# GpSimd makes the high and low parts of the score maxima, first in its step, from two buffers of raw maxima

## The chip, the cores and the metric

One Trainium2 chip, one of its cores. The metric is the device time of one execution, in microseconds (us). Engines are named as in the profile: PE is TensorE, DVE is VectorE, ACT is ScalarE, POOL is GpSimd, SP is SyncE, which here only issues DMAs.

## The reference

A cross-attention block with an MLP, for 8 batches of 256 query rows and 256 context rows, width 512, 16 heads of 32, all in fp32:

```python
x = layer_norm(hidden_states, ln1_w, ln1_b)
q = x @ q_w + q_b                       # 16 heads of 32
k = encoder_hidden_states @ k_w + k_b
v = encoder_hidden_states @ v_w + v_b
attn = softmax(where(mask, q k^T * scale, min), axis=-1)
hidden = (attn v) @ cproj_w + cproj_b + residual
y = gelu(layer_norm(hidden, ln2_w, ln2_b) @ fc_w + fc_b)    # width 2048
return hidden + y @ proj_w + proj_b
```

## The kernel before

The kernel keeps fp32 precision by splitting each operand into a high and a low part and multiplying in three passes (high by high, high by low, low by high). It has two stages. The first does attention for all batches and takes about the first half of the span; the second does the MLP in four chunks of 512 rows and doesn't touch what is changed.

The attention stage is one software pipeline, written out by hand for each engine. A step (it, g) belongs to batch `it` and to group g of four heads, G = 4*it + g; there are 32 groups. Every engine runs the same list of steps in order, and they meet only by semaphores. Within a step the engines work on different groups:

- PE projects queries and keys of group G+3 (`project_qk`, lines 975 to 977), multiplies the scores of group G+2 with queries on the partitions (`scores`, L1009), turns the maxima of group G+1 (`transpose_max`, L1093), multiplies the scores of group G again with keys on the partitions and the row maxima subtracted (`transposed_scores`, L993), and multiplies probabilities by values for group G-1 (`values`, L1080 and L1082).
- DVE reduces the scores of group G+2 to negated row maxima, one reduction a head into `negm` (`maximum`, L731). After the fourth head it makes the high part in fp32r of those eight numbers a partition (a cast, L736) and the low part (a subtraction, L738), both into `m12`. `m_lo_done` tells PE.
- ACT takes the exponentials twice, once in fp32 into `p32` (L533) and once in fp16 into `p_hi` (L535), and copies the turned maxima to `mrow` (`maxima_out`, L574), which SP's queue then stores as three rows under the queries. `transposed_scores` of the next step waits for that DMA.
- POOL subtracts the two exponentials to `p_lo` (L462, four a step, which `values` of the next step waits for). ACT may be two of them ahead of POOL. At the end of the step with g = 1 POOL also adds the output bias to the two hidden tiles of the next batch (L470); between the second and the third `p_lo` come the attention output's division by the row sums (L455, g = 0) and the inverse standard deviation (L423, g = 2).

PE's order inside a step is what matters here. For g = 1, 2 and 3 `transpose_max` stands directly behind `project_qk` and the first pair of `transposed_scores`; for g = 0 it stands behind `values`, the context's transposes and the first scores. PE executes strictly in order, so whatever `transpose_max` waits for holds the rest of the step.

Of the kernel before, what the change touches and what calls it, by code (L numbers as in the profile page):

```python
# [29 lines left out]
fp32 = mybir.dt.float32  # L30
# [4 lines left out]
ALU = mybir.AluOpType  # L35
# [4 lines left out]
def xattn_kernel(nc, x, ctx_in, mask, ln1_w, ln1_b, q_w, q_b, k_w, k_b, v_w, v_b, c_w, c_b,  # L40
# [5 lines left out]
    P = 128  # L46
    KT = D // P
    TT = LQ // P
    KC = LK // P
    GH = P // HD  # L50
    NG = H // GH
# [16 lines left out]
    with ctx:  # L68

        def sb(name, shape, dt, offset):  # L70
            return nc.alloc_sbuf_tensor_at(name, shape, dt, offset=offset)
# [41 lines left out]
        vb_bc = sb("vb_bc", [P, D], fp32, A4 + 4 * KB)  # L113
        cb_bc = sb("cb_bc", [P, D], fp32, A4 + 6 * KB)
        A5 = A4 + 8 * KB
        negm = sb("negm", [P, TT, GH], fp32, A5)
        m12 = sb("m12", [P, TT, 3 * GH], fp32r, A5 + 32)
        rl = sb("rl", [P, TT, H], fp32, A5 + 160)
        mrow = sb("mrow", [3 * GH, LQ], fp32r, A5 + 288)
# [23 lines left out]
        psum = ctx.enter_context(nc.psum_tensor("psum", [P, 8, 512], fp32))  # L143
        ST, MX, PV, MS = 0, 2, 4, 6
# [21 lines left out]
        s = {n: ctx.enter_context(nc.semaphore(n)) for n in names}  # L166
# [6 lines left out]
        def wait(eng, sem, value):  # L173

            if not isinstance(value, int) or value > 0:
                eng.wait_ge(s[sem] if isinstance(sem, str) else sem, value)
# [4 lines left out]

        def group(G):
            return not isinstance(G, int) or 0 <= G < GROUPS

# [6 lines left out]
        def emptied(it, kind, n):  # L191

            if kind in ("qk", "m"):
                G = it * NG + n + (3 if kind == "qk" else 1)
                if not group(G):
                    return None
                return ("qk_lo_done", (G + 1) * 2) if kind == "qk" else ("mrow_ready", G + 1)
            b = it + {"v": 1, "att": -1, "c": -1 - n, "x": 2, "ctx": 1}[kind]
# [60 lines left out]

        def fills_upto(G, parity):  # L260

            if isinstance(G, int):
                return (G // 2 + 1) * FILLS if G >= 0 else 0
            return (G - parity) * (FILLS // 2) + FILLS
# [136 lines left out]
        @block.gpsimd  # L401
        def _(pool):
            def small(dst, src, sem):
                with nc.allow_non_contiguous_dma(reason="per-partition vectors, a few KB"):
                    pool.dma_start(dst, src).then_inc(s[sem], 16)

            def column(v):
                return v.rearrange("(k p) -> p k", p=P)

            def repeated(v):  # L410
                return v.rearrange("(o n) -> o n", o=1).to_broadcast([P, D])

            pool.memset(ident[:, :], 0.0).then_inc(s["ident_zero"], 1)
            pool.wait_ge(s["ident_zero"], 1)
            pool.affine_select(out=ident[:, :], in_=ident[:, :], compare_op=ALU.not_equal, fill=1.0,
                               base=0, pattern=[[-1, P]], channel_multiplier=1).then_inc(s["ident_ready"], 1)
            pool.memset(mhalf[:, :], -0.5).then_inc(s["pool_consts"], 1)
            pool.wait_ge(s["pool_consts"], 1)

            def inverse_std(b, n, var_sem, out_sem):  # L420

                wait(pool, var_sem, b + 1)
                pool.tensor_tensor(rstd[:, 0:n], vareps[:, 0:n], mhalf[:, 0:n], ALU.pow).then_inc(s[out_sem], 1)  # L423

            def constants():
                pool.memset(m12[:, :, :].bitcast(fp32), 0.0).then_inc(s["pool_consts"], 1)
                pool.memset(vparts[:, :, :, 0:1], 1.0).then_inc(s["pool_consts"], 1)
                pool.memset(maskrow[:, 0, :], 1.0).then_inc(s["pool_consts"], 1)
                pool.wait_ge(s["pool_consts"], 4)
                pool.memset(kst[3 * HD:3 * HD + 3, :, :].bitcast(fp32), 1.0).then_inc(s["pool_consts"], 1)  # L430
                pool.wait_ge(s["pool_consts"], 5)
                small(vb_bc[:, :], repeated(v_b), "small_loaded")
                small(cb_bc[:, :], repeated(c_b), "small_loaded")
                split_weight_lo(3)
                for dst, src in ((cols[:, LN2W:LN2W + KT], ln2_w), (cols[:, LN2B:LN2B + KT], ln2_b),
                                 (cols[:, FCB:FCB + FT], fc_b)):
                    small(dst, column(src), "mlp_columns_loaded")

            def split_weight_lo(n):

                pool.wait_ge(s["w_hi_act"], n - 1)
                pool.tensor_tensor(w_att[:, n, 1, :, :], w_att_raw[:, n, 1, :, :], w_att[:, n, 0, :, :].bitcast(fp32),
                                   ALU.subtract).then_inc(s["w_lo_pool"], 1)

            def step(it, g):
                G = it * NG + g
                for u in range(4):
                    if u == 2 and g == 2 and batch(it + 2):
                        inverse_std(it + 2, TT, "ln_var", "ln_rstd")
                    if u == 2 and g == 0 and batch(it - 1):  # L450
                        b = it - 1
                        wait(pool, "pv_taken", (b + 1) * 16)
                        for t in range(TT):
                            a = att[:, t, :].rearrange("p (h d) -> p h d", h=H)
                            pool.tensor_tensor(a, a, rl[:, t, :].rearrange("p (h o) -> p h o", o=1).to_broadcast([P, H, HD]),  # L455
                                               ALU.mult).then_inc(s["att_normed"], 1)
                    if group(G):

                        wait(pool, "p_hi_done", (G * 4) + (u + 1))
                        wait(pool, "pv_mm", (G - 1) * 2)  # L460
                        slot = (g % 2) * 4 + u
                        pool.tensor_tensor(p_lo[:, slot, :], p32[:, u % 2, :], p_hi[:, slot, :],  # L462
                                           ALU.subtract).then_inc(s["p_lo_done"], 1)
                if g == 1 and batch(it + 1):
                    b = it + 1
                    wait(pool, "x_normed", (b + 1) * 2)
                    wait(pool, "small_loaded", SMALL)
                    for t in range(TT):
                        h = hidden_tile(b * TT + t)
                        pool.tensor_tensor(h, h, cb_bc[:, :], ALU.add).then_inc(s["cb_added"], 1)  # L470

            def ln2(j):
                inverse_std(j, 1, "y_var", "y_rstd")

            def tail(it, g):
                if (it, g) == (B - 2, 3):
                    ln2(0)
                if it == B - 1 and g < 3:
                    ln2(g + 1)

            iterations(pool, step, weights=constants, tail=tail)

            def pb(j):
                wait(pool, "y_normed", j + 1)
                h = hidden_tile(j)
                pool.tensor_tensor(h, h, pb_bc[:, :], ALU.add).then_inc(s["pb_added"], 1)

            pool.wait_ge(s["pb_loaded"], 16)
            for t in range(CH):
                pb(t)  # L490

            def body(c, first):
                if has_next(c):
                    for t in range(CH):
                        ln2(c * CH + (CH + t))
                        pb(c * CH + (CH + t))

            chunks(pool, body)
# [194 lines left out]
        def _(dve):  # L693
# [28 lines left out]
            def maximum(it, g, heads):  # L722
                G = it * NG + g + 2
                if not group(G):
                    return
                if heads[0] == 0:
                    wait(dve, "m_lo_done", G)
                for h in heads:
                    n = G * 4 + h
                    wait(dve, "max_mm", n + 1)  # L730
                    dve.tensor_reduce(out=negm[:, :, h:h + 1], in_=psum[:, MX + h % 2, :].rearrange("p (t k) -> p t k", t=TT),  # L731
                                      axis=AX.X, op=ALU.max, negate=True).then_inc(s["max_taken"], 1)
                if heads[-1] == GH - 1:
                    wait(dve, "max_taken", (G + 1) * 4)
                    wait(dve, "m_tr", G)
                    dve.tensor_copy(m12[:, :, GH:2 * GH], negm[:, :, :]).then_inc(s["m_hi_done"], 1)  # L736
                    wait(dve, "m_hi_done", G + 1)
                    dve.tensor_tensor(m12[:, :, 2 * GH:3 * GH], negm[:, :, :], m12[:, :, GH:2 * GH].bitcast(fp32),  # L738
                                      ALU.subtract).then_inc(s["m_lo_done"], 1)

            def statistics(b, tiles, stats_sem, mv_sem, var_sem):
                n = len(tiles)
# [487 lines left out]
```

## Time and profile before

| | |
|---|---|
| median of 3 runs | 763.83 us (758.85 to 768.42) |
| profiled execution | 762.24 us, its span 760.4 us, mean granted clock 0.971 |
| PE busy | 700.5 us (92% of the span) |
| DVE busy | 464.7 us (61%) |
| ACT busy | 321.7 us (42%) |
| POOL busy | 251.7 us (33%) |
| attention stage | up to about 400 us, some 42.6 to 44.4 us a batch |

Busy time is summed over instructions. A row of the timeline gives the start, the length, and in brackets the engine's idle time just ahead of it with what ended that; an instruction that waited for something has no bracket if its engine was idle for less than 0.15 us.

### The profile page before, as it was taken

How to read it: one execution, taken by the hardware profiler on the slowest of the kernel's cores; microseconds unless marked ns; L12 is line 12 of the kernel's file. 1: busy time of each engine (PE TensorE's matmuls, PEld its weight loads, DVE VectorE, ACT ScalarE, POOL GpSimd, SP SyncE). 2: the span in 40 equal slices, each digit the busy share in tenths (PEclk: the TensorE clock that was granted, in tenths of full speed). 3: DMA queues.
4: the chain of work that ended last, by engine and by line, in shares of the span. 5: the costliest groups of instructions: out<-in, count | busy, mean ns of one | idle time of the engine just before them, and what ended most of it. 6: DMA issues, size and time to landing. Idle time of an engine off the chain costs nothing.

```text
span 760.4 us, 13145 instructions
## 1 busy us (share of the span) xinstructions
PE 700.5 (92%) x4544; PEld 607.7 (80%) x4544; DVE 464.7 (61%) x860; ACT 321.7 (42%) x581; POOL 251.7 (33%) x217
## 2 busy tenths in 40 slices
PE   2789989899999989899689999999999999999998
PEld 2678879798888979798567888888888888888886
DVE  5567978978888888978858675432225233251213
ACT  4337766767676676857652211112211121211110
POOL 3505556655646656656653111000000001000000
PEclk9888989999999999999889999999999999999999
DMA  9655654644555554444604400010001000010001
GB/s 249 209 168 142 169 163 127 174 114 149 147 167 140 154 157 123 112 129 141 181 1 149 142 1 1 1 55 1 1 0 56 0 0 0 0 55 1 1 0 57
DMA packets 51130, 69.16 MB, mean 91 GB/s; under 512 B 8328, under 2 KB 29192, under 8 KB 51088
## 3 DMA queue, kind: packets, MB, share of 16 engines
q1 hardware_dynamic: 50816, 68.07, 30.9%
q0 software_dynamic: 272, 0.54, 0.3%
q8 instruction: 25, 0.41, 0.2%
q14 instruction: 17, 0.14, 0.1%
HBM read 47.21 MB, written 20.99 MB: 90 GB/s over the span
## 4 chain that ended last, share of the span: by engine, by line
PE 71%; issue 9%; DVE 8%; POOL 6%; DMA 3%; ACT 2%; SPq 0%; DVEq 0%; ACTq 0%; POOLq 0%
PE psum L1172 8%; PE psum L1174 8%; PE psum L1173 8%; PE psum L1159 8%; PE psum L1158 8%; PE psum L1157 8%; PE psum L975 5%; PE psum L976 5%; PE psum L977 5%; POOL p_lo L462 5%; PE psum L1059 3%; PE psum L1009 2%; PE psum L993 2%; DVE negm L731 2%; DVE xn L833 1%
## 5 line engine op out<-in xcount | busy, mean ns | idle before, releaser
L462 POOL TENSOR_TENSOR p_lo<-p,p_hi 128x512 f16<-128x512 f32 x128 | 157.1, 1236 | 135.6 <-ACT p_hi L535 135.1
L662 ACT ACTIVATE h<-psum,cols 128x512 f32<-128x512 f32 x64 | 44.1, 690 | 290.1 <-PE psum L1159 290.0
L913 DVE CAST h_hi<-h 128x512 fp32r<-128x512 f32 x64 | 27.6, 431 | 207.4 <-ACT h L662 207.4
L533 ACT ACTIVATE p<-psum,maskbias 128x512 f32<-128x512 f32 x128 | 88.3, 690 | 44.8 <-PE psum L993 42.7
L1172 PE MATMUL psum<-w_mlp,h_hi 128*128 128x512 f32 x256 | 100.8, 394 | 0.9 <-DVE hidden L758 0.9
L1174 PE MATMUL psum<-w_mlp,h_lo 128*128 128x512 f32 x256 | 99.7, 390 | 0.0
L1173 PE MATMUL psum<-w_mlp,h_hi 128*128 128x512 f32 x256 | 99.7, 389 | 0.0
L1157 PE MATMUL psum<-y_hi,w_mlp 128*128 128x512 f32 x256 | 99.7, 389 | 0.0
L1159 PE MATMUL psum<-y_hi,w_mlp 128*128 128x512 f32 x256 | 99.6, 389 | 0.0
L1158 PE MATMUL psum<-y_lo,w_mlp 128*128 128x512 f32 x256 | 99.6, 389 | 0.0
L535 ACT ACTIVATE p_hi<-psum,maskbias 128x512 f16<-128x512 f32 x128 | 88.7, 693 | 0.0
L731 DVE TENSOR_REDUCE negm<-psum 128x2 f32<-128x512 f32 x128 | 81.5, 678 | 2.7 <-PE psum L1009 2.2
L423 POOL TENSOR_TENSOR rstd<-vareps,mhalf 128x1 f32<-128x1 f32 (+1 forms) x24 | 16.0, 669 | 179.1 <-DVE vareps L751 179.1
L1172 PEld LDWEIGHTS psum<-w_mlp,h_hi 128*128 128x128 f32 x256 | 48.1, 188 | 10.9 <-issue 1.3
L1174 PEld LDWEIGHTS psum<-w_mlp,h_lo 128*128 128x128 f32 x256 | 48.1, 188 | 10.1
L1158 PEld LDWEIGHTS psum<-y_lo,w_mlp 128*128 128x128 f32 x256 | 48.1, 188 | 10.0
L1159 PEld LDWEIGHTS psum<-y_hi,w_mlp 128*128 128x128 f32 x256 | 48.1, 188 | 10.0
L1157 PEld LDWEIGHTS psum<-y_hi,w_mlp 128*128 128x128 f32 x256 | 48.0, 188 | 10.0
L1173 PEld LDWEIGHTS psum<-w_mlp,h_hi 128*128 128x128 f32 x256 | 48.1, 188 | 9.6
L1009 PE MATMUL psum<-stacks 97*128 97x256 f32 x256 | 47.2, 307 | 8.4 <-DMA stacks<-qk_rows 6.1
L993 PE MATMUL psum<-stacks 99*128 99x256 f32 x256 | 44.4, 293 | 5.8 <-ACT p_hi L535 5.7
L1080 PE MATMUL psum<-vparts,p_hi 128*128 128x97 bf16 x512 | 45.1, 213 | 2.3 <-POOL p_lo L462 2.3
(104 smaller groups left out, 1511.3 us busy)
## 6 DMA issues: line engine op xcount, KB each, us to landing
qk_rows<-qk SPq DMA_DIRECT2D x32, 512.0 KB, 2.7
stacks<-qk_rows SPq DMA_DIRECT2D x64, 256.0 KB
stacks<-qk_rows SPq DMA_DIRECT2D x64, 128.0 KB
hidden<-in_x_dram SPq DMA_DIRECT2D x8, 512.0 KB, 4.4
ctx_sb<-in_ctx_dram SPq DMA_DIRECT2D x8, 512.0 KB, 5.1
w_mlp_raw<-in_L_xattn_fc_w_dram SPq DMA_DIRECT2D x16, 256.0 KB, 4.6
w_mlp_raw<-in_L_xattn_proj_w_dram SPq DMA_DIRECT2D x16, 256.0 KB, 6.3
out_dram<-hidden SPq DMA_DIRECT2D x16, 256.0 KB, 2.1
```

The source lines that it names most:

```text
L462: pool.tensor_tensor(p_lo[:, slot, :], p32[:, u % 2, :], p_hi[:, slot, :], ALU.subtract).then_inc(s["p_lo_done"], 1)
L533: act.activation(p32[:, u % 2, :], psum[:, ST + kc, :], ACT.Exp, bias=maskbias[:, kc:kc + 1], scale=SCALE32)
L535: act.activation(p_hi[:, (g % 2) * 4 + u, :], psum[:, ST + kc, :], ACT.Exp, bias=maskbias[:, kc:kc + 1], scale=SCALE32).then_inc(s["p_hi_d ...
L731: dve.tensor_reduce(out=negm[:, :, h:h + 1], in_=psum[:, MX + h % 2, :].rearrange("p (t k) -> p t k", t=TT), axis=AX.X, op=ALU.max, negate ...
L993: ins = nc.tensor.matmul(psum[:, ST + kc, hh * LQ:(hh + 1) * LQ], kst[0:SUBROWS, h, kc * P:(kc + 1) * P], qst[0:SUBROWS, h, :], start=True ...
L1009: ins = nc.tensor.matmul(psum[:, MX + hh % 2, t * LK:(t + 1) * LK], qst[0:MAXROWS, h, t * P:(t + 1) * P], kst[0:MAXROWS, h, :], start=True ...
L1157: nc.tensor.matmul(bank, w[:, 0, :], y_hi[:, k, :], start=(k == 0), stop=False)
L1158: nc.tensor.matmul(bank, w[:, 0, :], y_lo[:, k, :], start=False, stop=False)
L1159: ins = nc.tensor.matmul(bank, w[:, 1, :], y_hi[:, k, :], start=False, stop=(k == KT - 1))
L1172: nc.tensor.matmul(acc, h_hi[:, f % 2, cut], w_mlp[f][:, 2, :], start=(f == 0), stop=False)
L1173: nc.tensor.matmul(acc, h_hi[:, f % 2, cut], w_mlp[f][:, 3, :], start=False, stop=False)
L1174: nc.tensor.matmul(acc, h_lo[:, f % 2, cut], w_mlp[f][:, 2, :], start=False, stop=(f == FT - 1)).then_inc(s["proj_mm"], 1)
```

## The change

The two instructions that make the high and the low part go from the end of DVE's `maximum` to POOL, as the first thing of its step (`split_maxima`), so in the step after the one in which the maxima were taken. The high part is now an addition of `negm` to the first four columns of `m12`, which are zero since the start, instead of a cast. `negm` becomes two buffers, by the parity of the group, and DVE's wait before it overwrites one of them is for the group two back. PE's wait for `m_lo_done` is unchanged, and so is its place.

```diff
-        negm = sb("negm", [P, TT, GH], fp32, A5)
+        negm = [sb(f"negm{i}", [P, TT, GH], fp32, A5 + 128 * i) for i in range(2)]
...
+            def split_maxima(it, g):
+
+                G = it * NG + g + 1
+                if group(G):
+                    wait(pool, "max_taken", (G + 1) * 4)
+                    wait(pool, "m_tr", G)
+                    pool.tensor_tensor(m12[:, :, GH:2 * GH], negm[(g + 1) % 2][:, :, :], m12[:, :, 0:GH].bitcast(fp32),
+                                       ALU.add).then_inc(s["m_hi_done"], 1)
+                    wait(pool, "m_hi_done", G + 1)
+                    pool.tensor_tensor(m12[:, :, 2 * GH:3 * GH], negm[(g + 1) % 2][:, :, :], m12[:, :, GH:2 * GH].bitcast(fp32),
+                                       ALU.subtract).then_inc(s["m_lo_done"], 1)
+
             def step(it, g):
                 G = it * NG + g
+                split_maxima(it, g)
                 for u in range(4):
...
                 if heads[0] == 0:
-                    wait(dve, "m_lo_done", G)
+                    wait(dve, "m_lo_done", G - 1)
                 for h in heads:
                     n = G * 4 + h
                     wait(dve, "max_mm", n + 1)
-                    dve.tensor_reduce(out=negm[:, :, h:h + 1], in_=psum[:, MX + h % 2, :].rearrange("p (t k) -> p t k", t=TT),
+                    dve.tensor_reduce(out=negm[g % 2][:, :, h:h + 1], in_=psum[:, MX + h % 2, :].rearrange("p (t k) -> p t k", t=TT),
                                       axis=AX.X, op=ALU.max, negate=True).then_inc(s["max_taken"], 1)
-                if heads[-1] == GH - 1:
-                    wait(dve, "max_taken", (G + 1) * 4)
-                    wait(dve, "m_tr", G)
-                    dve.tensor_copy(m12[:, :, GH:2 * GH], negm[:, :, :]).then_inc(s["m_hi_done"], 1)
-                    wait(dve, "m_hi_done", G + 1)
-                    dve.tensor_tensor(m12[:, :, 2 * GH:3 * GH], negm[:, :, :], m12[:, :, GH:2 * GH].bitcast(fp32),
-                                      ALU.subtract).then_inc(s["m_lo_done"], 1)
```

## Rows read from the trace of the kernel before

**Rows 1.** Windows of one batch each: busy times of the engines, granted clock, DMA.

```profile
core 0: us, PE busy (x) PEld busy (x) DVE busy (x) ACT busy (x) POOL busy (x), PEclk, DMA share, GB/s
203.71:246.31 42.60, 39.64 (x370) 36.53 (x369) 37.35 (x71) 30.48 (x55) 25.59 (x22) 1.00 0.53 150
246.31:289.04 42.73, 39.78 (x370) 36.56 (x369) 37.47 (x71) 30.58 (x55) 25.58 (x22) 1.00 0.53 149
289.04:333.44 44.40, 41.40 (x370) 38.05 (x369) 37.53 (x71) 30.69 (x55) 25.62 (x22) 0.96 0.43 121
```

**Rows 2.** Waits of PE from 246 to 290 us: total us, times, longest.

```profile
PE psum L1093 <- DVE m L738: 1.7, 1, 1.7
PE psum L975 <- DVE cs L798: 0.8, 1, 0.8
PE psum L1009 <- DMA stacks<-qk_rows: 0.2, 1, 0.2
PE psum L1059 <- DVE hidden L758: 0.2, 1, 0.2
```

**Rows 3.** The tile of the parts: duration in ns, shortest, median and longest.

```profile
L736 DVE CAST m<-negm x32: 171/678/1071, 42.8 to 371.1; 128x8 fp32r<-128x8 f32 x32
L738 DVE TENSOR_TENSOR m<-negm,m x32: 166/1068/1126, 43.0 to 371.8; 128x8 fp32r<-128x8 f32 x32
```

**Rows 4.** Timeline of POOL in the batch from 246 us.

```profile
246.54 2.52 POOL L470 TENSOR_TENSOR hidden<-hidden,cb_bc 128x512 f32 x2
249.01 2.30 POOL L462 TENSOR_TENSOR p_lo<-p,p_hi 128x512 f16<-128x512 f32 x2
252.37 0.70 POOL L423 TENSOR_TENSOR rstd<-vareps,mhalf 128x2 f32<-128x2 f32 x1 [1.06 <-DVE vareps L751]
253.28 2.32 POOL L462 TENSOR_TENSOR p_lo<-p,p_hi 128x512 f16<-128x512 f32 x2 [0.20 <-ACT p_hi L535]
...
263.84 2.32 POOL L462 TENSOR_TENSOR p_lo<-p,p_hi 128x512 f16<-128x512 f32 x2 [3.60 <-ACT p_hi L535]
...
275.15 3.05 POOL L462 TENSOR_TENSOR p_lo<-p,p_hi 128x512 f16<-128x512 f32 x2
279.64 1.16 POOL L462 TENSOR_TENSOR p_lo<-p,p_hi 128x512 f16<-128x512 f32 x1 [1.44 <-ACT p_hi L535]
```

**Rows 5.** Timeline of DVE in the same batch.

```profile
252.12 0.17 DVE L751 TENSOR_SCALAR vareps<-mv 128x2 f32<-128x2 f32 x1
...
254.50 1.12 DVE L738 TENSOR_TENSOR m<-negm,m 128x8 fp32r<-128x8 f32 x1
...
269.69 0.69 DVE L798 TENSOR_TENSOR cs<-psum,cs 128x512 fp32r<-128x512 f32 x1 [0.78 <-ACT cs L542]
...
277.71 1.27 DVE L731 TENSOR_REDUCE negm<-psum 128x2 f32<-128x512 f32 x2
...
279.22 0.17 DVE L738 TENSOR_TENSOR m<-negm,m 128x8 fp32r<-128x8 f32 x1
```

**Rows 6.** Timeline of PE in the same batch: the turning of the maxima.

```profile
246.79 0.38 PE L1093 MATMUL psum<-ident,m 128*12 128x128 f32 x2
...
255.81 0.38 PE L1093 MATMUL psum<-ident,m 128*12 128x128 f32 x2
...
269.34 0.38 PE L1093 MATMUL psum<-ident,m 128*12 128x128 f32 x2
...
279.53 0.38 PE L1093 MATMUL psum<-ident,m 128*12 128x128 f32 x2 [1.69 <-DVE m L738]
```

**Rows 7.** Timeline of POOL elsewhere: instructions of other sizes.

```profile
11.36 0.75 POOL L405 DMA_DIRECT2D vb_bc<-in_L_xattn_v_b_dram  x1 [0.31 <-POOL stacks L430]
26.52 4.55 POOL L442 TENSOR_TENSOR w_att<-w_att_raw,w_att 128x2048 fp32r<-128x2048 f32 x1 [13.87 <-ACT w_att L515]
...
354.10 0.56 POOL L423 TENSOR_TENSOR rstd<-vareps,mhalf 128x1 f32<-128x1 f32 x1 [2.25 <-DVE vareps L751]
```

**Rows 8.** Waits of PE from 10 to 60 us.

```profile
PE psum L1009 <- DMA stacks<-qk_rows: 2.4, 1, 2.4
```

**Rows 9.** Windows: PE's busy time and granted clock behind that wait.

```profile
35.00:45.00 10.00, 9.11 (x50) 0.83 0.50 134
```

## The prediction

> **What bounds the kernel now.** I read the profile from the coarse to the fine. The table of busy times says PE, with 92% of the span. A window for each batch of the attention stage says the same there: 39.8 us of PE in a batch of 42.73 us, DVE 37.5, POOL 25.6 [rows 1]. So what PE doesn't wait for now can't be won. PE's waits in that batch add up to about 3 us, and only one of them, 1.7 us, has to do with the edited instructions [rows 2]. The two instructions look dear on DVE: the cast has a median of 0.68 us and the subtraction of 1.07 us, but their shortest are 0.17 each [rows 3]. The long ones end together with an instruction of POOL: the subtraction that starts at 254.50 ends at 255.62, when POOL's pair of low parts that started at 253.28 ends, at 255.60 [rows 4, 5]. They are stretched, not large. Some 0.68 + 1.07 - 2 x 0.17 = 1.4 us of DVE a step is such stretching, but DVE spends it at the end of a step in which nobody but PE's turning of the maxima waits for it.
>
> The third reading is a race: for each of the four steps of a batch, when PE gets to the turning of the maxima, when the last maximum is there, and when POOL comes free of the step before. I take the batch from 246.31 to 289.04; the two batches ahead of it show the same pattern to 0.1 us.
>
> **The change, part by part.**
>
> *DVE's two instructions leave.* In the steps with g = 2 and g = 3 DVE next works on what PE projects, and idles for it already, so nothing is won. In the step with g = 0 DVE would start about a microsecond earlier, but it waits again at 269.69 for ACT's context high part (0.78 us of idle) [rows 5], which follows PE; the lead is lost there, before the value split and the maxima that make PE's 1.7 us wait. I take nothing.
>
> *The price of the pair on POOL.* The trace has no small addition on POOL. From above: the power of two numbers a partition takes 0.70 us, of one 0.56 [rows 4, 7], and between an instruction of POOL and one that waits for it lie up to 0.31 us [rows 7]; with 0.25 between, that makes 1.65 us for the pair. From below: 2048 elements of subtraction take 4.55 us [rows 7], 512 of addition take 2.52/2 = 1.26 us [rows 4], so a line through them has a slope of 2.14 ns an element and begins at 0.16 us; two of 0.15 and 0.05 between make 0.35 us. Power is another operation and addition is the same one, so I take the value near the lower end: 0.20 + 0.15 + 0.20 = 0.55 us. PE starts 0.14 us after the low part is done (279.39 to 279.53) [rows 5, 6]. A gain from the pair itself is excluded: DVE's undisturbed pair takes 0.41 us, from 278.98 to 279.39 [rows 5], and starts without waiting for POOL.
>
> A rule of the Trainium skill speaks against this part of the change: "GPSIMD Engine Reference", section "Engine selection", gives elementwise work to VectorE, since GpSimd is about twice as slow with two inputs. Taken on DVE's undisturbed 0.17 us it would make the pair 2 x 0.34 + 0.15 = 0.83 us, an estimate by that page, and the sum below 19 x 0.28 = 5.3 us larger. It lies between my two ends, and the trace has no row that decides it.
>
> *The place: first in POOL's step, so behind everything of the step before.* Each step apart:
>
> - g = 2. POOL ends the step before with the two bias additions of the hidden tiles and comes free at 249.01; PE turned the maxima at 246.79 [rows 4, 6]. Now it can at 249.01 + 0.55 + 0.14 = 249.70, which is 2.91 us later. All seven batches that have these additions (g = 2 of batches 0 to 6) show it alike: 7 x 2.91 = 20.4 us.
> - g = 3. POOL comes free at 253.28 + 2.32 = 255.60; the turning goes from 255.81 to 255.60 + 0.69 = 256.29, 0.48 us [rows 4, 6]. POOL's third and fourth low parts follow PE's second pair of scores, so the distance stays even after the stall of g = 2. 7 x 0.48 = 3.4 us.
> - g = 0. POOL comes free at 263.84 + 2.32 = 266.16, PE turns at 269.34 [rows 4, 6]. Hidden, by 2.5 us.
> - g = 1. POOL is free at 275.15 + 3.05 = 278.20, ahead of the last maximum at 277.71 + 1.27 = 278.98 [rows 4, 5]. POOL starts 0.08 us after DVE's semaphore (252.29 to 252.37) [rows 4, 5], so PE turns at 278.98 + 0.08 + 0.55 + 0.14 = 279.75 instead of 279.53, 0.22 us. This race is open only from batch 2 on: 5 x 0.22 = 1.1 us.
>
> Sum of the stalls: 24.9 us. PE holds everything behind the turning: the values, the next scores, their maxima and the projections. ACT's copy of the turned maxima comes after the exponentials anyway, and SP's queue holds the fills of the stacks behind that copy's store, but both move by less than PE. Since PE stands still meanwhile, its waits for a fill and for DVE's hidden tile (0.2 and 0.2 us a batch [rows 2]) should vanish: 6 x 0.4 = 2.4 us back. POOL's queue has the low parts behind the new wait; at g = 1 they start at 279.64 after 1.44 us of idle [rows 4], and move by 0.1 us at most. The second buffer and DVE's earlier wait cost nothing: the old wait never showed as DVE's idle time. The tail, the last batch and the MLP chunks I take as unchanged.
>
> *The clock.* The last two batches shown differ by 44.40 - 42.73 = 1.67 us, at a clock of 0.96 against 1.00 and equal work [rows 1]: one fall to the lower level (1.2 of 2.4 GHz) costs 1.7 us. In the start of the kernel PE waited 2.4 us for a fill and the clock of the stretch behind it was 0.83 [rows 8, 9]. The 1.7 us wait at g = 1 was followed by a fall in the batch from 289 us and not in the two ahead of it. A stall of 2.9 us is longer than any of these, so I count a fall behind each: 7 x 1.7 = 11.9 us.
>
> A rule of the Trainium skill that speaks for the change: what DVE shows as 0.17 alone and 1.07 beside POOL, the page "Advanced Engine Details and Errata", "VectorE Performance Modes", puts to a port of DVE that is shared with POOL. The trace agrees. By that rule the release of DVE would be worth some 1.4 us in each of 32 steps if DVE bounded the stage; it doesn't, so it changes no term here.
>
> **The rivals.**
>
> *No fall of the clock.* The stalls come, but PE's clock stays. 762.24 + 24.9 - 2.4 = 784.7 us, and 781 with the shorter pair (19 turnings x 0.2 = 3.8 less). For it: two of the three batches shown took 1.7 us without a fall. Against it: the start of the kernel, and the length.
>
> *The pair is as slow as the power.* 1.1 us more at 19 turnings is 20.9 us, so 817.5 us. For it: the only small two-input instructions on POOL in the trace are 0.56 and 0.70 us. Against it: the line through the larger sizes.
>
> *PE's slack takes it.* If the fills, the accumulating products and the maxima are ahead of PE by more than the rows show, later steps run faster after a stall and half of it is lost: about 770 to 778 us. Against it: PE is 93% busy in the batch, and its other waits are 1.2 us.
>
> *The other side: DVE is the hidden bound.* The 1.7 us wait at g = 1 ends a chain through DVE (context low part, value split, maxima). If the microsecond released at the end of the step before got through that chain, PE would win up to 1.2 us in five batches, and the clock falls of two of them: 762 - 6 - 3.4 = some 753 us. It decides only where POOL is free before the last maximum, and that is so at g = 1 alone; at g = 2 POOL comes free 2.2 us after PE's turning whatever DVE does, so this needs the additions of the hidden tiles to be hidden too. Nothing in the rows says so. That the change fails to move the pair to POOL isn't possible; the additions with zero give the same numbers.
>
> **How the numbers follow.** Forecast, with the execution profiled: 762.24 + 24.9 - 2.4 + 11.9 = 796.6 us, say 796; it lies 1.6 us under the median of the runs shown, which is small beside the terms. Its own range is 788 to 806, for pairs of 0.35 to 0.9 us and five to eight falls; chance 0.50. No fall: 0.25. Slow pair: 0.11. Slack: 0.10. Faster: 0.04. The range from 778 to 816 leaves out the other side, the deeper half of the slack and the end of the slow pair. A change of less than 2% (under 779 and over 748 us) is about what a measurement of this kernel can't tell from none: chance 0.11. Slower by more: 0.86. Faster by more: 0.03.
>
> **What would show it.** In the profile after: 19 delayed turnings; a wait of PE's L1093 for POOL, some 2.9 us long in each of seven batches and about 0.5 in another step of each; batches of about 47 to 48 us; no wait at g = 0; POOL's new pair at 0.2 us each, directly behind L470 at g = 2; a clock under 0.97 in each batch; DVE's busy time in a batch about 5 us less, with no gain on PE. The prediction is wrong if POOL's small instructions cost 0.5 us or more, if the clock holds, or if PE catches up within the batch.

## The result

The changed kernel takes 794.0 us (median of 4 runs, 792.56 to 795.46); the kernel before takes 762.65 us (median of 4, the three above and one more). The ratio is 1.038, with a 95% interval from 1.034 to 1.043: slower by about 31 us. The forecast was 796 us. The profiled execution has a span of 790.8 us against 760.4.

In the page of the changed kernel, the table of busy times:

```profile
PE 708.5 (90%) x4544; PEld 613.0 (78%) x4544; DVE 434.1 (55%) x796; ACT 323.0 (41%) x581; POOL 271.3 (34%) x281
```

DVE has lost 64 instructions and 31 us of busy time, POOL has gained 64 and 20 us. PE runs the same 4544 products in 8 us more, and stands still for 22 us more. Those two numbers are the whole loss.

Windows of one batch each, to be laid beside [rows 1]:

```profile
216.45:263.28 46.83, 41.12 (x370) 37.57 (x369) 33.84 (x62) 30.63 (x55) 28.04 (x30) 0.96 0.48 136
263.28:311.88 48.60, 42.89 (x370) 39.37 (x369) 34.10 (x62) 30.75 (x55) 28.06 (x30) 0.93 0.46 131
311.88:358.55 46.67, 41.05 (x370) 37.64 (x369) 33.83 (x62) 30.69 (x55) 27.99 (x30) 0.96 0.40 115
```

A batch took 42.6 to 42.7 us where the clock held, and takes 46.7 to 48.6. The third field in front of the clock shows that DVE is 3.4 us less busy, and nobody is better off. PE's waits in the batch from 263.28 us, beside [rows 2]:

```profile
PE psum L1099 <- POOL m L454: 4.4, 2, 2.6
PE psum L981 <- DVE cs L804: 0.8, 1, 0.8
PE psum L1065 <- DVE hidden L764: 0.3, 1, 0.3
```

Line 1099 is the turning of the maxima. Its wait was for DVE, 1.7 us, once a batch; now it is for POOL, 4.4 us in two waits. The same batch in the timeline of POOL, beside [rows 4]:

```profile
263.50 2.49 POOL L483 TENSOR_TENSOR hidden<-hidden,cb_bc 128x512 f32 x2
265.95 0.21 POOL L451 TENSOR_TENSOR m<-negm,m 128x8 fp32r<-128x8 f32 x1
266.24 0.20 POOL L454 TENSOR_TENSOR m<-negm,m 128x8 fp32r<-128x8 f32 x1
266.40 2.27 POOL L475 TENSOR_TENSOR p_lo<-p,p_hi 128x512 f16<-128x512 f32 x2
...
300.19 0.20 POOL L451 TENSOR_TENSOR m<-negm,m 128x8 fp32r<-128x8 f32 x1 [0.85 <-DVE negm L744]
300.47 0.20 POOL L454 TENSOR_TENSOR m<-negm,m 128x8 fp32r<-128x8 f32 x1
```

and in the timeline of PE, beside [rows 6]:

```profile
266.50 0.38 PE L1099 MATMUL psum<-ident,m 128*12 128x128 f32 x2 [2.58 <-POOL m L454]
...
277.37 0.38 PE L1099 MATMUL psum<-ident,m 128*12 128x128 f32 x2
...
300.82 0.50 PE L1099 MATMUL psum<-ident,m 128*12 128x128 f32 x2 [1.86 <-POOL m L454]
```

DVE's last two maxima ahead of the first of these pairs are

```profile
260.36 1.29 DVE L744 TENSOR_REDUCE negm<-psum 128x2 f32<-128x512 f32 x2
```

At g = 2 the pair is ready to go when the last maximum is there, at 261.65 us, but POOL has low parts and then the bias additions of the hidden tiles ahead of it until 265.95. The pair itself takes 0.49 us. PE turns the maxima 0.06 us later, and had nothing to do for 2.58 us.

How late a turning is can be read against the start of PE's first scores of the same step, which doesn't depend on the pair. The windows above and those of [rows 1] begin at these scores, so at g = 2 the distance is 246.31 to 246.79 before and 263.28 to 266.50 now. From the timelines of PE at the steps with g = 2, 3 and 1, these distances were 0.48, 0.48 and 2.33 us, and are 3.22, 0.77 and 2.49. That is 2.74, 0.29 and 0.16 us more, at 7, 7 and 5 turnings: 19.2 + 2.0 + 0.8 = 22.0 us.

### The profile page after: what moved, and what is told of

It reads as the page before. It is cut to its first block, busy times and chain, and to the rows that moved or that the text cites. A ratio compares the mean times of both kernels' runs of the same rounds, so it can differ in the third digit from the quotient of the medians.

```text
span 790.8 us, 13144 instructions
## 1 busy us (share of the span) xinstructions
PE 708.5 (90%) x4544; PEld 613.0 (78%) x4544; DVE 434.1 (55%) x796; ACT 323.0 (41%) x581; POOL 271.3 (34%) x281
## 4 chain that ended last, share of the span: by engine, by line
PE 60%; issue 16%; POOL 9%; DVE 9%; ACT 3%; DMA 3%; SPq 0%; POOLq 0%; DVEq 0%; ACTq 0%
PE psum L1178 7%; PE psum L1180 7%; PE psum L1179 7%; PE psum L1163 7%; PE psum L1165 7%; PE psum L1164 7%; POOL p_lo L475 6%; PE psum L981 3%; PE psum L983 3%; PE psum L982 3%; POOL hidden L483 2%; DVE negm L744 2%; DVE vparts L851 2%; PE psum L1015 2%; DMA stacks<-qk_rows 1%
## 5 line engine op out<-in xcount | busy, mean ns | idle before, releaser
L1015 PE MATMUL psum<-stacks 97*128 97x256 f32 x256 | 50.1, 320 | 7.4 <-DMA stacks<-qk_rows 6.3
L778 DVE SCALAR_TENSOR_TENSOR qk<-psum,cols,qk 128x256 fp32r<-128x256 f32 x64 | 28.0, 478 | 52.4 <-ACT qk L579 52.3
L1086 PE MATMUL psum<-vparts,p_hi 128*128 128x97 bf16 x512 | 49.7, 222 | 2.2 <-POOL p_lo L475 2.2
```

The lines of the kernel that those rows point to most:

```text
L1015: ins = nc.tensor.matmul(psum[:, MX + hh % 2, t * LK:(t + 1) * LK], qst[0:MAXROWS, h, t * P:(t + 1) * P], kst[0:MAXROWS, h, :], start=True ...
L1086: nc.tensor.matmul(o, p_hi[:, slot, cut], vparts[:, kc, GH * gp + hh, :], start=(kc == 0), stop=False)
```

## The experiments

The time from the start of the kernel to batch 0 differs by up to 4.5 us between profiled executions whatever the kernel, and I haven't traced why. Where a microsecond matters I therefore compare the stretch between the same two events of the timeline: the start of the first scores with keys on the partitions in group 2, and the same in group 28. Before:

```profile
73.87:351.58 277.71, 258.00 (x2358) 0.98 0.50 144
```

The fields are the stretch, its length, PE's busy time and its granted clock. The changed kernel:

```profile
74.94:381.23 306.29, 267.63 (x2358) 0.94 0.46 131
```

28.6 of the 30.4 us by which the spans differ lie in this stretch, and PE is busy for 9.6 us more with the same 2358 products.

Two cautions hold for everything below. The kernel before was timed again beside each set of experiments, with medians of 766.51 (15 runs), 766.3 (29) and 767.15 us (16), some 4 us over the 762.65 us of the result; the changed kernel was timed only then. Each ratio is to the kernel before in the same set. And a trace is of one run, which can lie several us from the median of its kernel; where it does, I say so.

**The place: bias additions behind the pair.**

```diff
             def step(it, g):
                 G = it * NG + g
                 split_maxima(it, g)
+                if g == 2 and batch(it + 1):
+                    b = it + 1
+                    wait(pool, "x_normed", (b + 1) * 2)
+                    wait(pool, "small_loaded", SMALL)
+                    for t in range(TT):
+                        h = hidden_tile(b * TT + t)
+                        pool.tensor_tensor(h, h, cb_bc[:, :], ALU.add).then_inc(s["cb_added"], 1)
                 for u in range(4):
...
-                if g == 1 and batch(it + 1):
...
```

> The changed kernel with one thing moved: GpSimd's two bias additions of the hidden tiles stand behind the new pair (first thing of the step with g = 2) instead of ahead of it (last thing of the step with g = 1). Theory, the place: POOL comes free 2.5 us earlier, so the turning at g = 2 is late by 0.3 us instead of 2.7; 7 x 2.4 = 17 us of stall and some 10 us of clock falls go, and the time is 764 to 768 us, within 1% of the kernel before. Rival, the engine: small instructions on POOL, or POOL and DVE getting into each other's way, are the cost; then moving the additions gives back less than half, and the time stays over 780 us.

Measured 772.73 us, ratio 1.010 (1.006 to 1.013) to the kernel before. POOL's timeline and the stretch:

```profile
250.34 2.32 POOL L482 TENSOR_TENSOR p_lo<-p,p_hi 128x512 f16<-128x512 f32 x2 [3.19 <-ACT p_hi L548]
252.62 0.20 POOL L451 TENSOR_TENSOR m<-negm,m 128x8 fp32r<-128x8 f32 x1
252.90 0.20 POOL L454 TENSOR_TENSOR m<-negm,m 128x8 fp32r<-128x8 f32 x1
253.19 2.53 POOL L466 TENSOR_TENSOR hidden<-hidden,cb_bc 128x512 f32 x2
...
77.39:360.77 283.38, 260.94 (x2359) 0.97 0.51 142
```

The pair stands ahead of the additions, and the stretch is 283.4 us: 22.9 of the 28.6 us are gone. The same instructions run on the same engines, so the engine is not the cause; what POOL has to do first is. What is left is 5.7 us. The 0.3 us at g = 2 and g = 3, the 0.16 at g = 1 and one more fall of the clock would make 6.5; the difference isn't traced. The median is 5 us over the upper end of what I expected; the kernel before took 766.51 us beside it, where I had worked from 762.65, and that accounts for 4 of them.

**The buffer alone.**

```diff
-                    wait(dve, "m_lo_done", G)
+                    wait(dve, "m_lo_done", G - 1)
...
-                    dve.tensor_copy(m12[:, :, GH:2 * GH], negm[:, :, :]).then_inc(s["m_hi_done"], 1)
+                    dve.tensor_copy(m12[:, :, GH:2 * GH], negm[g % 2][:, :, :]).then_inc(s["m_hi_done"], 1)
```

The diff is against the kernel before; the maxima and the low part use the same buffer.

> The kernel before with the doubled buffer of the raw maxima and DVE's earlier wait, and the pair left on DVE. Theory: the second buffer frees nothing that anyone waits for, so the time is that of the kernel before within 0.3%. Rival: the old wait held the first maximum of each step; then this alone is faster by up to 32 x 0.1 = 3 us.

Measured 766.01 us, ratio 1.000 (0.996 to 1.003). By itself the second buffer brings nothing that can be told from the noise, and at most 2.8 us; it only makes room for the pair to be late. The stretch:

```profile
75.99:355.55 279.56, 258.78 (x2358) 0.98 0.51 143
```

That is 1.9 us more than in the trace of the kernel before, at the same time of the whole: differences of 2 us between two traces of this stretch mean nothing.

**The price of the pair: twice.**

```diff
                     wait(pool, "m_tr", G)
+                    pool.tensor_tensor(m_spare[:, :, 0:GH], negm[(g + 1) % 2][:, :, :], m12[:, :, 0:GH].bitcast(fp32),
+                                       ALU.add).then_inc(s["spare_hi"], 1)
+                    wait(pool, "spare_hi", G + 1)
+                    pool.tensor_tensor(m_spare[:, :, GH:2 * GH], negm[(g + 1) % 2][:, :, :], m_spare[:, :, 0:GH].bitcast(fp32),
+                                       ALU.subtract).then_inc(s["spare_lo"], 1)
+                    wait(pool, "spare_lo", G + 1)
```

> The changed kernel with the pair done twice on POOL, first into a spare tile and then as before, at the same place. Theory: POOL is what the turning waits for in 19 steps, so each is later by one more pair of 0.56 us (0.20 + 0.08 + 0.20 + 0.08), 10.6 us, and a few more falls of the clock of 1.7 us: 803 to 812 us. Rival, POOL isn't the last (PE waits for something else that ends with it): no change from 794.

Measured 812.71 us, ratio 1.062 (1.059 to 1.066). The stretch:

```profile
77.27:406.09 328.82, 280.57 (x2358) 0.89 0.43 122
```

PE's stall at g = 2 grows from 2.58 to 3.14 us, at g = 3 by 0.56 and at g = 1 by 0.55: each of the 19 turnings moves by exactly one pair, so all of them are bound by POOL. That is 10.6 us. The stretch is 22.5 us longer than the changed kernel's; the rest of that is the clock, now at 0.89, with PE busy for 12.9 us more. But this trace is of the slowest of the five runs, 5.1 us over the median. The medians lie 18.7 us apart, which leaves some 8 us for the clock; which of the two prices is the larger can't be told from this. The median is 0.7 us over the range that I expected.

**The clock by itself: PE is kept busy during the stall.**

```diff
                 if g == 2:
+                    if not isinstance(it, int) or 0 <= it < B - 1:
+                        wait(pe, "pv_taken", (it * NG + g - 2) * 4 + 2)
+                        for i in range(22):
+                            nc.tensor.matmul(psum[:, PV, GH * VW:GH * VW + 120], w_att[:, 2, 0, 0, 0:P],
+                                             w_att[:, 2, 0, 0, 0:120], start=True, stop=True)
                     transpose_max(it, g)
```

> The changed kernel with 22 matrix products of 120 columns, whose result nobody reads, ahead of the turning at g = 2 in batches 0 to 6, to keep PE busy in the 2.6 us in which it waits for POOL; they wait for nothing that is late. Theory, the clock: the stall itself stays, the falls that came with it in the trace of the changed kernel (a loss of some 10 us over the stage) go, so 784 to 788 us although PE does more. Rival, the clock cost nothing of its own (the falls would lie where PE has slack): 794, or more if the products last longer than the stall.

Measured 788.82 us, ratio 1.029 (1.024 to 1.034) against 1.038 (1.034 to 1.043) without the products. That is 0.8 us over the range that I expected and 5 us under the rival's; the two intervals just touch, so the trace has to decide. PE's timeline at one g = 2 and the stretch:

```profile
265.01 0.64 PE L999 MATMUL psum<-stacks 99*128 99x256 f32 x4
265.49 2.57 PE L1134 MATMUL psum<-w_att 128*128 128x120 f32 x22
268.25 0.39 PE L1099 MATMUL psum<-ident,m 128*12 128x128 f32 x2 [0.20 <-POOL m L454]
...
78.36:378.53 300.17, 278.81 (x2513) 0.97 0.48 133
```

PE executes 7 x 22 products more, starts each turning as late as the changed kernel does, and is 6.1 us faster over the stretch, with the clock at 0.97 instead of 0.94. The two are the same kernel but for the activity in the gap. The clock can be laid side by side: 10 us from the start of the first scores with keys on the partitions, in one step with g = 2, in the changed kernel, with the products, and with the pair done twice:

```profile
263.28:273.28 10.00, 7.42 (x61) 0.83 0.47 126
```

```profile
265.01:275.01 10.00, 9.80 (x96) 1.00 0.45 127
```

```profile
279.01:289.01 10.00, 6.86 (x52) 0.66 0.37 110
```

The granted clock is the same in all seven steps with g = 2 of each kernel: 0.83 with a gap of 2.58 us, 0.66 with one of 3.14 us, and 1.00 where the gap is filled. So the fall that comes with the stall has a price of its own, and where the stall was 0.56 us longer the loss of clock was double. The gain is somewhat under the 10 us that I expected: falls of the clock follow the 1.85 us waits at g = 1 in four of five batches here, and in two of five in the changed kernel.

**PE's order: the values fill the wait.**

```diff
                 if g == 2:
-                    transpose_max(it, g)
                     values(it, g)
+                    transpose_max(it, g)
...
                 if g == 3:
-                    transpose_max(it, g)
                     values(it, g)
+                    transpose_max(it, g)
```

> The changed kernel with PE's order alone altered: at g = 2 and g = 3 the values (some 1.2 us of PE) stand ahead of the turning of the maxima, where they fill the wait for POOL. Theory: the stall at g = 2 falls from 2.6 to about 1.4 us and the one at g = 3 goes, 7 x 1.5 = 10.5 us, and part of the clock falls with it: 776 to 784 us. Rival: the values or what follows the turning come late instead (the maxima's rows, the fills behind them), and the time stays within 3 us of 794.

Measured 772.67 us, ratio 1.010 (1.007 to 1.013), better than expected. The turning's row at g = 2 and the stretch:

```profile
255.12 0.38 PE L1099 MATMUL psum<-ident,m 128*12 128x128 f32 x2 [1.39 <-POOL m L454]
...
74.23:360.08 285.85, 254.65 (x2359) 0.99 0.49 139
```

The stall is 1.39 us, and the clock is at 0.99: in none of the seven steps with g = 2 did it fall. (The traced run is the fastest of the ten, 3.3 us under the median; its mean clock is 0.978, that of the others 0.969 to 0.978.) With POOL as late as in the changed kernel, 20.4 of the 28.6 us are gone: 7 x 1.19 = 8.3 us of stall at g = 2, 0.9 at g = 3 and 13.0 us of PE's busy time, less 1.9 us of longer waits for DVE's hidden tile. So the second condition of the loss is that nothing that PE could do stands in front of the turning.

**The tail.**

```diff
-            def tail(it, g):
-                if (it, g) == (B - 2, 3):
-                    ln2(0)
-                if it == B - 1 and g < 3:
-                    ln2(g + 1)
...
                 split_maxima(it, g)
+                if isinstance(it, int) and it == B - 1:
+                    ln2(g)
```

> The changed kernel with POOL's inverse standard deviations of the MLP's norm in the last batch put behind the new pair instead of ahead of it, because they wait for DVE and PE stood 4.2 us at the turning behind one of them. Theory from the step times: the last batch and what follows take only 0.8 us more in the changed kernel than before, so this stall lies where DVE is late anyway, and the time stays within 1.5 us of 794. Rival, the stall counts: 3 to 5 us less.

Measured 790.79 us, ratio 1.034 (1.028 to 1.040). In the changed kernel the longest single stall is in the last batch. PE's waits from 380 to 405 us:

```profile
PE psum L1099 <- POOL m L454: 6.0, 2, 4.2
```

POOL's inverse standard deviation for the MLP's norm is the last thing of a step there; it waits for DVE's statistics, and the pair is queued behind it. From the end of the stretch to the first product of the MLP's second matrix it is, in the changed kernel and in this one:

```profile
381.23:438.69 57.46, 44.42 (x333) 0.88 0.29 80
```

```profile
380.59:434.97 54.38, 43.36 (x333) 0.91 0.31 85
```

3.1 us less, where I had expected none and the rival 3 to 5. The intervals of the two ratios overlap, but three more traces have the inverse standard deviation ahead of the pair and PE's order as it was, those with the additions moved, the pair twice and the products in the gap; they took 58.4, 57.8 and 57.6 us for this piece. Against all four the gain is 3.1 to 4.0 us. The rival was right, and my argument that DVE is late there anyway was wrong. The kernel before and the one with the buffer alone took 56.7 and 54.7 us, so what the change costs in the tail is between 0.8 and 3.7 us, and no run here settles it closer.

**What the pair on DVE costs.** Two kernels made from the one before.

```diff
                 if g == 1:
+                    values(it, g)
                     transpose_max(it, g)
                     scores(it, g, (0, 1))
                     for j in range(2):
                         transposes(it, "att", j, it - 1, att, "att_normed", 2, "att_tr")
-                    values(it, g)
                     project_v(it, 0)
```

> The kernel before, with PE's values ahead of the turning of the maxima at g = 1, where PE waits 1.7 us for DVE's last maximum in five batches. Theory: the wait falls to some 0.4 us, 5 x 1.3 = 6.5 us, and the two clock falls behind it may go: 0.988 to 0.992 of the time before. Rival: PE's wait is only moved to the scores or to the transposes behind it, which wait for the same maxima: no change.

Measured 760.43 us, ratio 0.993 (0.991 to 0.996), a little less than expected. The turning waits no more. PE's waits over the stretch:

```profile
PE psum L975 <- DVE att_t L852: 6.1, 6, 1.1
PE psum L975 <- DVE cs L798: 4.0, 5, 0.8
PE psum L1080 <- POOL p_lo L462: 2.5, 5, 0.5
```

and the stretch:

```profile
77.82:352.64 274.82, 255.42 (x2358) 0.99 0.52 145
```

8.4 us of waiting for the maxima have become 6.1 for DVE's low part of the attention output and 2.5 for POOL. The wait was only moved, as the rival had it; of the 2.9 us that the stretch is shorter, 2.6 are PE's busy time, with a clock of 0.99 instead of 0.98.

```diff
-        negm = sb("negm", [P, TT, GH], fp32, A5)
-        m12 = sb("m12", [P, TT, 3 * GH], fp32r, A5 + 32)
+        m12 = [sb(f"m12_{i}", [P, TT, 3 * GH], fp32r, (A5 + 32, A5 + 544 + 3 * KB)[i]) for i in range(2)]
...
-                    dve.tensor_reduce(out=negm[:, :, h:h + 1], in_=psum[:, MX + h % 2, :].rearrange("p (t k) -> p t k", t=TT),
+                    dve.tensor_reduce(out=m12[g % 2][:, :, GH + h:GH + h + 1], in_=psum[:, MX + h % 2, :].rearrange("p (t k) -> p t k", t=TT),
                                       axis=AX.X, op=ALU.max, negate=True).then_inc(s["max_taken"], 1)
-                if heads[-1] == GH - 1:
...
-                wait(pe, "m_lo_done", G + 1)
+                wait(pe, "max_taken", (G + 1) * 4)
```

> The kernel before with no pair on any engine: DVE's maxima are written rounded straight into the high columns of a doubled tile, and the low part is left at zero (the softmax is the same whatever is subtracted). It shows what taking the pair off DVE can bring at most, with nothing given to POOL. Theory: PE's wait at g = 1 is shorter by the pair, 5 x 0.4 = 2 us, and the tail by a microsecond or two: 0.994 to 0.998 of the time before. Rival, DVE as the hidden bound: 9 us or more, 0.988 or less.

Measured 759.82 us, ratio 0.993 (0.990 to 0.995), a little more than the 0.994 to 0.998 that I expected and less than the rival's 0.988. This is the most that taking the pair off DVE can bring when nobody gets it: 0.5 to 1%. PE's wait for the maxima at g = 1 is 1.3 us instead of 1.7.

**The change with its places mended.** The two edits on POOL (additions and inverse standard deviations behind the pair) are those above, and so is PE's order at g = 2 and 3; at g = 1 it is

```diff
                 if g == 1:
+                    values(it, g)
                     transpose_max(it, g)
```

> The changed kernel with all its misplacements taken out at once: the bias additions and the last batch's inverse standard deviations behind the pair, and PE's values ahead of the turning at g = 1, 2 and 3. Theory: with the place mended the pair on POOL costs next to nothing and gains next to nothing, so the time is that of the kernel before with values first at g = 1: 0.993 to 0.999 of the time before. Rival: the pair on POOL still costs 0.3 us a turning wherever it stands (the low parts behind it come late): 1.002 or more.

Measured 760.76 us, ratio 0.994 (0.991 to 0.996), as expected. The kernel before with the values first at g = 1 and the pair on DVE has 0.993. So in the time of the whole the pair on POOL, well placed, costs nothing and brings nothing, to within some 2 us. The stretch is not quite as even:

```profile
75.42:353.14 277.72, 256.25 (x2358) 0.99 0.51 144
```

That is 2.9 us longer than with the pair on DVE. PE waits there 3.8 us for the fills of the stacks instead of 1.6, and 3.5 for POOL's low parts instead of 2.5; the pieces ahead of the stretch and behind it are shorter by as much. With one trace of each, and 1.9 us between two that should agree, this may be a small cost or none. Nor is the comparison free of a second difference: the values first at g = 2 and 3 were not tried with the pair on DVE.

**No pair and PE's order.** The kernel with the maxima straight into the high columns, and in it

```diff
                 if g == 1:
+                    values(it, g)
                     transpose_max(it, g)
```

> The kernel before with no pair on any engine (the maxima rounded straight into the high columns, the low part zero) and PE's values ahead of the turning at g = 1. Theory: both shorten the same wait of 1.7 us, so together they bring 1 to 2 us more than either: 0.988 to 0.993 of the time before. Rival: independent gains that add up, 0.986.

Measured 759.37 us, ratio 0.992 (0.989 to 0.994). This and the three others at 0.993 to 0.994 beat both kernels, and can't be told from each other. The two gains don't add up: that would have been 0.986, outside the interval. The 1 to 2 us that I expected beyond either alone are 0.5 and 1.1 us here, less than the intervals resolve.

## Why the prediction was right

*Stalls.* I had 20.4 + 3.4 + 1.1 = 24.9 us and the traces show 19.2 + 2.0 + 0.8 = 22.0. The race of the four steps held in each: g = 0 without a wait, seven long stalls at g = 2, a small one at g = 3, and 1.85 instead of 1.70 us at g = 1. The terms that were a little too large are PE's start behind the low part, 0.06 us at g = 2 instead of 0.14, and the pair, 0.49 instead of 0.55 us. Of the signs that I named, the wait at g = 2 is 2.58 us and not 2.9; at g = 3 PE sits idle for only 0.13 us, though the turning is 0.29 us later. The line through the larger sizes gave its price almost exactly (0.20 us for each instruction); the power of one or two numbers, at 0.56 and 0.70, was the wrong neighbour, and so was twice DVE's time, the 0.83 us of the prediction's estimate. Doubling the pair showed that each turning costs 0.56 us a pair.

*Clock.* 11.9 us were forecast, as seven falls. In the changed kernel a fall came with each of the seven stalls at g = 2. PE's busy time over the stretch rose by 9.6 us; one fall of those that the kernel before had in batch 1 is missing. Here the experiment with products in the gap shows cause, not only company: 6.1 us less with more work, and a clock of 1.00 in place of 0.83 behind all seven gaps. No fall came with the waits of 1.4 us in the kernel with PE's order changed, and one with those of about 1.85 us at g = 1 in one to four of the five batches of a run. That each of the seven longer stalls would bring exactly one fall was an extrapolation from a single wait of 2.4 us in other surroundings; that it came out so is in part luck, since 3.14 us brought twice the loss.

*Given back.* 2.4 us were forecast from two waits. The stretch shows that the 2.4 us for the fills of the stacks went, and that the 1.0 us for DVE's hidden tile became 1.5. With the stalls and the clock that makes 22.0 + 9.6 - 2.4 + 0.5 = 29.7 us, 1.1 more than the stretch grew; where that went isn't traced. In the whole, 34.4 us were forecast over the execution profiled and the two profiled executions differ by 30.3.

*The tail* was taken as unchanged, and that was wrong by 0.8 to 3.7 us. I had read the edit for the steady step alone. POOL's list has another instruction at the end of the last batch's steps, one that waits for DVE, and the rule by which I had found the bias additions (what stands at the end of the step before?) finds it as well.

*DVE's release.* Forecast at nothing: the waits of others for DVE outside the pair didn't get shorter. It was a little more than nothing at most, 0.5 to 1% when POOL doesn't take the pair. DVE's busy time fell by 3.4 us a batch and not by 5, for a reason that stands below. The rival on the other side was the one that I priced at 9 us; its largest possible value, with the pair gone altogether, measured 6.5 us.

The two steps that carried the forecast were right for their reason: moving the additions alone took back 22.9 of 28.6 us.

## What to carry to other kernels

A busy time that is stretched by another engine is no saving: look at who waits for the end of it. Before an instruction goes first in another engine's step, read what is last in that engine's step before, in every form of the step, the last iteration's too; that is what it will wait for. And where an in-order PE is the bound, price a stall twice: once for its length and once for the clock behind it, and look for work that can stand ahead of the wait.

## What the runs showed of the hardware

The blocking between DVE and POOL goes both ways. In the changed kernel at g = 0, POOL's small addition takes 1.18 us instead of 0.20, and DVE's subtraction on two inputs in SBUF takes 2.10 us instead of the 1.22 of before (the medians of its eight instructions in either kernel). POOL's timeline and DVE's:

```profile
286.14 1.17 POOL L475 TENSOR_TENSOR p_lo<-p,p_hi 128x512 f16<-128x512 f32 x1
287.27 1.18 POOL L451 TENSOR_TENSOR m<-negm,m 128x8 fp32r<-128x8 f32 x1
```

```profile
286.29 2.10 DVE L886 TENSOR_TENSOR v<-v,v 128x1024 f32<-128x1024 f32 x1
```

DVE's begins while POOL works on a low part that ends at 287.31, and ends 2.10 us later, at 288.39; POOL's small one ends at 288.45. I read this as each having waited until the other was through: once the stretched instructions were gone from DVE's list, a later one was stretched instead. That is 0.9 us a batch, and more than half of the difference between the expected 5 and the measured 3.4 us of release. The Trainium skill, "GPSIMD Engine Reference", section "Key points", says that GpSimd shares its SBUF interfaces with VectorE, with contention when DVE's instruction is in a 2-port perf mode or has two SBUF inputs; the trace agrees, with both directions of it: 0.20 to 1.18 us on POOL, 1.22 to 2.10 us on DVE. It cost nothing in this place, since PE reaches the turning at g = 0 at 290.47 us, 1.7 us after the pair is done.
